# A four-layer graph network on one core: weight turns moved into the eigenvector steps, edge work shortened, unread products behind the solves

## The reference, cut to what matters

```python
def _L0_gnn_ref(features, A, W1, b1, g1, be1, W2, b2, g2, be2):
    ...
    h = jax.nn.relu(_batchnorm(x @ W1.T + b1, g1, be1))
    out = h @ W2.T + b2
    out = _batchnorm(out, g2, be2)
def _L1_gnn_ref(features, A, W1, b1, W2, b2):
    ...
    L_norm = d_inv_sqrt[:, None] * L * d_inv_sqrt[None, :]
    _, U = jnp.linalg.eigh(L_norm)
    agg = jnp.einsum('mn,bnd->bmd', U.T, features)
    h = jax.nn.relu(agg @ W1 + b1)
    out = h @ W2 + b2
    return jnp.einsum('nm,bmd->bnd', U, out)
x = _layernorm(x + _L0_gnn_ref(x, adj, ...))
x = _layernorm(x + _L1_gnn_ref(x, adj, ...))
x = _layernorm(x + _L2_gnn_ref(x, ..., adj, src, dst))   # attention over 256 edges
x = _layernorm(x + _L3_gnn_ref(x, adj, ...))             # two graph layers, four LSTMs
```

## Time and profile before

| what | value |
|---|---|
| median of 3 runs | 1051.76 us (1051.39 to 1053.5) |
| the profiled execution, its own time | 1054.46 us |
| span in its profile | 1052.3 us |
| PE busy | 944.5 us, 90% |
| DVE, ACT, POOL busy | 61%, 55%, 18% |
| mean granted PE clock | 0.915 |
| start to the first product of the solver (L522) | 35.16 us |
| transpose of the signed vectors (L707) | 432.81 us |

### The profile page before, as it was taken

How to read it: one execution, slowest core, us unless ns; L and a number is a source line. 1 busy time by engine, 2 the same in 40 slices (tenths; PEclk the granted TensorE clock), 3 DMA queues, 4 the chain that set the end, 5 groups by cost and what they waited for, 6 DMA issues and landing times.

```text
span 1052.3 us, 13417 instructions
## 1 busy us (share of the span) xinstructions
PE 944.5 (90%) x4009; PEld 614.2 (58%) x4009; DVE 637.0 (61%) x2168; ACT 577.3 (55%) x1480; POOL 186.9 (18%) x470
## 2 busy tenths in 40 slices
PE   3899988778888996999999999999999999999994
PEld 3555554454556664666888777885444466654442
DVE  5567676645658774477445797434544555554676
ACT  0566536645537773277644345436955655555556
POOL 0233333313333332000000000000011111110055
PEclk9699868866779896799999999999999999999998
DMA  9100000000000000000000000000000000000014
GB/s 260 41 1 1 1 0 2 1 1 1 2 0 2 1 1 1 1 1 1 1 1 1 1 2 1 1 1 1 1 0 0 1 1 0 1 1 0 1 40 121
DMA packets 14329, 13.00 MB, mean 12 GB/s; under 512 B 897, under 2 KB 11057, under 8 KB 14257
## 3 DMA queue, kind: packets, MB, share of 16 engines
q1 hardware_dynamic: 14018, 11.98, 4.0%
q10 hardware_dynamic: 238, 0.16, 0.1%
HBM read 7.89 MB, written 4.19 MB: 11 GB/s over the span
## 4 chain that ended last, share of the span: by engine, by line
PE 73%; DVE 16%; ACT 6%; issue 3%; POOL 1%; ACTq 0%; DVEq 0%; DMA 0%; POOLq 0%
PE bank L898 15%; PE bank L922 9%; PE bank L819 3%; PE bank L754 3%; PE bank L764 3%; PE bank L778 3%; PE bank L809 3%; PE bank L517 2%; PE bank L585 2%; PE bank L475 2%; PE bank L584 2%; PE bank L729 1%; PE bank L885 1%; PE bank L827 1%; PE bank L877 1%
## 5 line engine op out<-in xcount | busy, mean ns | idle before, releaser
L1364 ACT ACTIVATE hid_t<-bank,gate_b 128x512 f32<-128x512 f32 (+1 forms) x252 | 150.8, 631 | 67.9 <-PE bank L922 66.8
L922 PE MATMUL bank<-ms,w_t 128*128 128x512 f32 (+1 forms) x288 | 112.8, 535 | 6.9 <-DVE ms L2094 6.9
L1468 POOL COPY hid_t<-feat_t 128x1008 f32<-128x1008 f32 (+1 forms) x12 | 27.9, 2328 | 498.4 <-DVE feat_t L2090 498.4
L898 PE MATMUL bank<-hid_t,w_t 128*128 128x336 f32 (+1 forms) x296 | 106.5, 506 | 1.2 <-DVE x L2098 1.2
L898 PE MATMUL bank<-feat_t,w_t 128*128 128x512 f32 x208 | 93.1, 603 | 0.0
L922 PEld LDWEIGHTS bank<-ms,w_t 128*128 128x128 f32 x288 | 54.4, 192 | 56.6 <-issue 34.2
L898 PEld LDWEIGHTS bank<-hid_t,w_t 128*128 128x128 f32 x296 | 56.2, 191 | 46.1 <-issue 26.3
L1371 ACT ACTIVATE hid_t<-hid_t 128x512 f32<-128x512 f32 (+1 forms) x72 | 41.8, 581 | 52.3 <-DVE hid_t L2076 27.7
L898 PEld LDWEIGHTS bank<-feat_t,w_t 128*128 128x128 f32 x208 | 39.1, 189 | 51.0 <-issue 46.8
L1155 ACT ACTIVATE con<-bank,con 128x1 f32<-128x1 f32 x62 | 16.2, 261 | 90.7 <-PE bank L585 90.4
L1004 ACT ACTIVATE x<-x,perm 128x128 f32<-128x128 f32 x128 | 52.3, 482 | 2.6 <-DVE perm L1507 2.6
(11 more groups left out here) (421 smaller groups left out, 2110.2 us busy)
## 6 DMA issues: line engine op xcount, KB each, us to landing
...
```

What stands on the lines that cost most here:

```text
L898: return mm(bank[4 * u + BANK_OF[g]][:, 0:w], w_t[:, WB_IH + 4 * (it.p - 1) + g, :], lstm_x(n), start=True, stop=(it.k == 0))
L922: mm(bank[4 * u + BANK_OF[g]][:, 0:w], w_t[:, WB_HH + 4 * (it.p - 1) + g, :], lstm_h_of(it.chain)[:, 0:w], start=False, stop=True).then_in ...
L1364: f(dst[:, 0:w], bank[4 * u + BANK_OF[g]][:, 0:w], ACT.Tanh if g == G_G else ACT.Sigmoid, bias=gate_b[:, 4 * (it.p - 1) + g:4 * (it.p - 1) ...
```

## The change

- The weights lie in `feat_t` instead of `hid_t[0]`. SP issues the DMAs of the first group (`w0_loaded`), then `x`, then the other weights.
- PE turns group 0 alone in `edges`, behind the product with `adj` and the row sum. Groups 1 to 9 are turned in steps 18 to 22 by `TURN_AT`: two groups in each of 18 to 21, one in 22. ACT copies them in `behind_step` of the same step. Steps 18 to 22 are no longer in `QUIET`.
- DVE signals `edge_stored` after its first copy. Two copies go to ACT (`edge_act`). The masks `con_b`, `pen_f`, `pen_b` and the attention vector move to `head_rows`, at the head of layer 1.
- Every level of a solve is followed by one unread product (`kept_busy_beside`), five in turn 8 and six behind turn 15.
- The signs of the three splits are worked out side by side: 6 instructions for all three and 3 single ones. The five unread products there become two.

```diff
-QUIET, FULL_FROM = (18, 19, 20, 21, 22, 41, 42, 43, 60, 61, 62), 36
+QUIET, FULL_FROM = (41, 42, 43, 60, 61, 62), 36
+TURN_AT = {18: (1, 2), 19: (3, 4), 20: (5, 6), 21: (7, 8), 22: (9,)}
...
-        w_nat = hid_t[0]
+        w_nat = feat_t
...
-            for at_, src, k in blocks:
-                sp.dma_start(w_nat[:, at_:at_ + k, :], src).then_inc(s["w_loaded"], 16)
+            for at_, src, k in blocks[0:2]:
+                sp.dma_start(w_nat[:, at_:at_ + k, :], src).then_inc(s["w0_loaded"], 16)
             for k in range(4):
                 n = B // 4
                 sp.dma_start(x[:, k * n:(k + 1) * n, :], a["x"][k * n:(k + 1) * n].rearrange("b n d -> n b d")).then_inc(s["x_loaded"], 16)
+            for at_, src, k in blocks[2:]:
+                sp.dma_start(w_nat[:, at_:at_ + k, :], src).then_inc(s["w_loaded"], 16)
...
-            def weights_transposed():
-                pe.wait_ge(s["w_loaded"], 128)
...
+            def weights_transposed(g, k):
+
+                if g == 0:
+                    pe.wait_ge(s["w0_loaded"], 32)
+                if g == 1:
+                    pe.wait_ge(s["w_loaded"], 96)
+                    pe.wait_ge(s["l0_agg_sb"], TILES)
+                if g > 2:
+                    pe.wait_ge(s["wt_stored"], g - 1)
+                for b in range(TB):
+                    t = tr(bank[k][:, b * P:(b + 1) * P], w_nat[:, g * TB + b, :], ident)
+                t.then_inc(s["wt_turned"], 1)
...
+                for g in TURN_AT.get(slot, ()):
+                    weights_transposed(g, 3 - g % 2)
...
+            def kept_busy_beside(n):
+
+                if n == HALF:
+                    pe.wait_ge(s["x_ready"], CREDIT + TILES)
+                mm(bank[7][:, 0:3 * P], ident, w_t[:, WB_IH:WB_IH + 3, :], start=True, stop=True)
...
-                for _ in range(5):
+                for _ in range(2):
                     kept_busy(HALF)
...
+                act.wait_ge(s["edge_sorted"], 1)
+                f(dst_st[:, :], pa[1][:, 0:E], ACT.Copy)
+                f(src_s[:, :, :], ph[1][:, 0:E], ACT.Copy).then_inc(s["edge_act"], 1)
+                weights_stored(0, 4)
...
+                for g in TURN_AT.get(slot, ()):
+                    weights_stored(g, 3 - g % 2)
...
+                copy(src_st[:, :], pa[0][:, 0:E]).then_inc(s["edge_stored"], 1)
+                copy(dst_s[:, :, :], pm[1][:, 0:E])
                 link(copy(seg[:, 0:E], ph[0][:, 0:E]))
                 dve.memset(con_f[:, 0:1], 0.0)
                 link(tt(con_f[:, 1:E], seg[:, 1:E], seg[:, 0:E - 1], ALU.is_equal))
+                dve.wait_ge(s["edge_act"], 1)
+                link(tt(sum_st[:, :], src_st[:, :], dst_st[:, :], ALU.add))
```

67 lines of the change are left out of this document (28 added, 39 removed).

## The result

| | before | after |
|---|---|---|
| median of the runs, us | 1051.72 (1051.39 to 1054.19, 6 runs) | 1048.32 (1046.73 to 1049.62, 6 runs) |
| profiled execution: own time / span, us | 1054.46 / 1052.3 | 1049.02 / 1047.1 |
| mean granted clock of PE | 0.915 | 0.929 |
| ratio of after to before | | 0.9958, 95% interval 0.9946 to 0.9971 |

The changed kernel is faster by 3.4 us in the medians, 4.4 us by the ratio. The forecast was 7.3. The profiled span fell by 5.2 us; the profiled execution of the kernel before, 1054.46 us, lay 2.7 us above the median of its runs, so the profiles make the change look larger than the medians do.

The account below looks back on a forecast made before the run. PE was taken to bound the kernel (73% of the chain), with everything changed ahead of layer 1 counting fully. Terms -3.95 + 1.5 - 0.5 - 0.4 - 0.8 - 3.15 = -7.3 took 1051.76 to 1044.5 us, range 1039.5 to 1052.5.

Parts of the forecast that it names:

- The edges, -3.95: Edge work ahead of the solver: PE's product starts right behind the first copy, so `tmp` starts 3.95 us earlier.
- Rival 4: Front: edge indices or a table load come late, or layer 0 waits for `x`; edges' gain lost, 1048.4 us; chance 0.07.
- Steps 18 to 25, +1.5: Weight transposes and ACT copies replace unread products; step changes and a longer half clock cost 1.5 us, ends -3.5 and +5.
- The +5: Steps 18 to 25 if transposes hold no clock: +5 instead of +1.5, total 1048.0 us; chance 0.06.
- Turn 8, -0.5: Five unread products between turn 8's levels hold the clock in the first half only: -0.5 us, ends -4 and +2.
- Rival 3: The clock holds nearly everywhere; steps 18 to 25 gain 1.5, turn 8 gains 4; 1038 us; chance 0.13.
- The last solve, -0.4 and -0.8: Unread products raise the clock after two levels: 9.05 against 9.45 us, and the three following products gain 0.8.
- Rival 1: Last solve stays at half clock, +3.8 instead of -1.2; layer 1 starts slow, +1.7; 1051.2 us; chance 0.22.
- The signs, -3.15: Behind the last solve: nine fewer DVE instructions and two unread products start the signed vectors' transpose 3.15 us sooner.

Follow-up runs that it names:

- front_turn: Changed kernel without any unread product in the solves and with the signs as before (five products); ratio to the kernel before 0.9960.
- best2: Changed kernel plus four unread products before the last solve, more at the signs, bias rows turned late, unread pairs of steps 18, 20, 21, 22 back; ratio 0.9861.
- no_turn8: Changed kernel without the unread product behind each of turn 8's five levels; ratio to the kernel before 0.9978.
- cols_late: Changed kernel with the bias rows' transpose and DVE's two operations on it put later; ratio to the kernel before 0.9946.
- signs_only: Kernel before with only the three signs side by side and two unread products there instead of five; ratio to the kernel before 0.9998.
- after_again: The changed kernel measured a second time, as it is; ratio to the kernel before 0.9940.
- no_last: Changed kernel without the unread product behind each of the last solve's six levels; ratio to the kernel before 0.9918.
- entry_only: Changed kernel with four unread products ahead of the last solve and none behind its levels; ratio to the kernel before 0.9873.
- entry: Changed kernel with four more unread products in PE's waits ahead of the last solve; ratio to the kernel before 0.9887.
- last_two: Changed kernel with two unread products behind each level of the last solve instead of one; one execution, no ratio, solve 23.12 us.

## Why the prediction was right or wrong

1044.5 us was forecast, with a range of 1039.5 to 1052.5; 1048.32 came. Direction and range held. The centre was 3.8 us too low by the medians, 2.9 by the ratio and 1.0 by the second measurement.

- **The edges, -3.95.** The row of work shortened by 4.26, as worked out. What failed is the step that took 25.25 as the start of the first copy. Rival 4 had the cause in view (`x` ahead of other loads) and dismissed it, because `x` then lands earlier. But with `x` ahead, other loads landed later: PE waited 0.31 to 1.20 us for the bias rows in seven of nine profiles, and in neither of the two with the old order. -2.93 arrived in the first profile. In the nine profiles the solver's first product comes at 31.6 us in the mean, 3.7 sooner than in the mean of the two with the old front (35.16 and 35.53), so the term was off by less than the first profile says. That `x` is what delays the bias rows was not tested by itself: no kernel moved its DMAs back.
- **Steps 18 to 25, +1.5.** Steps 17 to 23 lost 3.11 us in the changed kernel's two profiles. Eight profiles have the same code up to turn 8: four lost 3.1 in these steps, the other four (front_turn among them, +1.43) 1.1 to 1.5. With steps 23 to 25, which the term covered too, it is +4.1 to +4.2 or +1.9 to +2.2. Behind them step 26 to 27 gained 1.8 to 1.9 in all eight, which the forecast did not have. The signs of the single steps were right: step 19 to 20 gained (7.51 to 4.97 or 5.88 us), step 20 to 21 lost (6.45 to 7.72 or more) and step 22 to 23 lost (5.04 to 6.83 or 6.96, best2 excepted). The clock rose late, as expected: it was 0.51 from 137 to 175 us. The +5 that the Trainium skill's rule would give (TensorE: Matmul & The Clock Gate, Part 4: PE-mode transpose) did not come, +4.2 at the most. No run here held transposes alone at the half clock, so the rule itself stays open.
- **Turn 8, -0.5.** The term was mis-sized. The reason given for the half ("idle for long pieces here even with them, so I expect the clock to hold in the first half only") was wrong: it held throughout, and 2.93 came. Rival 3's price of 4 was nearer.
- **The last solve, -0.4 and -0.8.** This step failed, and Rival 1 described what happened in the levels. "I expect it to rise after two levels" rested on one row, the five unread products behind the solve, where PE was filled with these alone. In a level the unread product shares PE with the solve's own products, and the clock did not rise in five levels (five profiles). The slow level was also 2.62 us and not 2.25. The forecast took 0.92 us from the level's start to the unread product and 1.3 for it; it was 1.04 (405.05 to 406.09) and 1.58 (to 407.67). Loss in the stretch: 2.20 + 3.3 of the signs = +5.5; without the products 5.3 of it came back.
- **The rule of unbroken work.** The Trainium skill (TensorE: Matmul & The Clock Gate, Why this matters for your kernels) says that TensorE reaches its full clock when it is kept busy without a pause. Here the trace disagrees: busy 14.95 of 15 us, granted 0.50, and 15.00 of 15 us at 0.50 in no_turn8 and cols_late. The measurement decides.
- **The signs, -3.15.** Right in place (3.3, and 3.1 alone), and worth nothing in sum. The forecast counted layer 1's slow head only in Rival 1, as a consequence of a slow solve. signs_only shows that dropping three of the five products is enough for it, with the solve as before. With products behind the levels the head was slow in two profiles and fast in three.
- **What was not in the sum.** Between the two profiles the touched stretches came to -0.55 us and the rest, mostly layer 1's head, to +2.15; the -6.80 that make it -5.2 came from stretches whose code is the same, and which differ in how PE's clock falls in them. So the total landed in the range partly by luck: in this pair of profiles what the change touches, layer 1's head included, lost 1.6 us. The prediction did say that the clock changes differ between executions, and the record bears it out. The kernels after, after_again, no_last, entry_only, entry, last_two, no_turn8 and front_turn have the same code up to turn 8. Their profiles fall into two groups:

| profiles | to step 0 | steps 0 to 17 | step 10 to 11 | steps 17 to 23 |
|---|---|---|---|---|
| after, after_again, no_last, entry_only | 34.71 to 35.15 | 98.19 to 98.46 | 9.99 to 10.05 | 40.51 to 40.55 |
| entry, last_two, no_turn8, front_turn | 33.24 to 34.47 | 96.36 to 96.79 | 5.78 | 38.50 to 38.85 |

What differs between these eight kernels runs only after these stretches. The group with the later start of step 0 is the slower one in both stretches; that the moment decides is argued from this order only.

The 4.47 us of steps 32 to 63 can be placed. Of 31 steps, 27 last the same within 0.4 us. Three are shorter and one is longer:

| step | before | after | both profiles of after agree? | other kernels |
|---|---|---|---|---|
| 32 to 33 | 6.81 | 4.66 | yes | 4.65 or 6.2 to 6.8 |
| 34 to 35 | 8.06 | 6.19 | yes | 6.2 or 8.06 |
| 52 to 53 | 7.08 | 5.11 | yes | 6.71 or 7.08 |
| 57 to 58 | 5.85 | 6.70 | yes | 5.84 to 5.91 |

The windows of the first two, before (two rows) and after (two rows), show the clock:

```profile
242.23:249.04 6.81, 6.25 (x21) 3.12 (x19) 3.54 (x15) 4.41 (x14) 2.38 (x7) 0.82 0.00 0
254.74:262.80 8.06, 8.06 (x23) 5.07 (x22) 3.77 (x16) 3.20 (x12) 1.76 (x6) 0.56 0.00 0
```

```profile
237.15:241.81 4.66, 4.09 (x19) 2.27 (x17) 3.55 (x15) 4.09 (x14) 2.38 (x7) 1.00 0.01 4
...
247.50:253.69 6.19, 6.04 (x24) 3.48 (x22) 3.77 (x16) 3.20 (x12) 1.76 (x6) 0.84 0.00 0
```

The work is the same, and PE is at 1.00 and 0.84 in place of 0.82 and 0.56. Why the clock falls there in one profile and not in another is not settled. no_last has the code of the changed kernel in all these steps, and its step 52 to 53 took 6.71 us and not 5.11. All kernels without turn 8's products have the longer steps 32 and 34, wherever turn 8 starts (from 211.6 us in no_turn8 to 218.7 in the kernel before). Of those with the products, the five in which turn 8 starts at 214.3 us or later have the shorter steps, and the five in which it starts at 213.3 or sooner have the longer ones. So the shorter steps came only with the products, and only with the later start. That the moment counts is read off these fourteen profiles; no run moved it by itself.
